# Up product of an MLP with its 192 channels as 128 + 64 contraction rows and the rests of two tiles in the two row halves of TensorE, and the projection bias added by GpSimd

## What is computed

```python
out = out.reshape(bw, WS, WS, DIM) @ proj_w + proj_b        # DIM = 192
out = window_unpartition(out, WS, pad_hw, (H, W))
x = shortcut + out
h2 = layernorm(x, n2_w, n2_b)
mlp = jax.nn.gelu(h2 @ lin1_w + lin1_b, approximate=False) @ lin2_w + lin2_b   # 192 -> 768 -> 192
return x + mlp
```

## Time and profile before

| | |
|---|---|
| three runs | 717.22, 715.27, 713.39 us, median 715.27 |
| the profiled execution | 715.34 us, of which 713.6 us from first to last instruction; TensorE's granted clock 0.979 on average |
| TensorE matmul | busy 642.6 us (90%), 5696 passes |
| TensorE weight loads | busy 492.6 us (69%), beside the matmuls |
| DVE, ACT, GpSimd | busy 359.8 (50%), 338.1 (47%), 112.8 us (16%) |
| up product, L544 | 192 passes, 87.1 us busy |

### The profile page before, as it was taken

How to read it: one execution, slowest core, us unless ns; L and a number is a source line. 1 busy time by engine, 2 the same in 40 slices (tenths; PEclk the granted TensorE clock), 3 DMA queues, 4 the chain that set the end, 5 groups by cost and what they waited for, 6 DMA issues and landing times.

```text
span 713.6 us, 14706 instructions
## 1 busy us (share of the span) xinstructions
PE 642.6 (90%) x5696; PEld 492.6 (69%) x5696; DVE 359.8 (50%) x982; ACT 338.1 (47%) x807; POOL 112.8 (16%) x156
## 2 busy tenths in 40 slices
PE   2889998999899989999999999999999977899996
PEld 2577757875787678767776777677767753676764
DVE  4466336633663466344734473547344713166665
ACT  3346543654365426542664266426642641254463
POOL 1500040004000400040004000400010021023130
PEclk9999999999999999999999999999999975999999
DMA  4673820085008400740073006300640000000000
GB/s 99 150 182 99 194 83 1 10 196 135 1 5 199 123 2 3 193 97 2 3 166 90 1 4 160 96 0 4 157 100 1 3 1 1 0 1 24 23 23 22
DMA packets 32954, 47.31 MB, mean 66 GB/s; under 512 B 5468, under 2 KB 13982, under 8 KB 32886
## 3 DMA queue, kind: packets, MB, share of 16 engines
q1 hardware_dynamic: 31654, 45.98, 26.5%
q10 hardware_dynamic: 1232, 0.40, 0.2%
HBM read 7.05 MB, written 1.57 MB: 12 GB/s over the span
## 4 chain that ended last, share of the span: by engine, by line
issue 58%; PE 22%; POOL 11%; DVE 5%; DMA 2%; ACT 2%; POOLq 0%; SPq 0%; ACTq 0%; DVEq 0%
PE bank L544 3%; POOL xn L735 3%; POOL q_nat L722 3%; PE bank L696 2%; PE bank L366 2%; POOL rstd L715 2%; PE bank L554 2%; PE bank L690 2%; PE bank L474 2%; PE bank L493 2%; POOL x_all L728 2%; PE bank L681 1%; PE bank L444 1%; PE bank L672 1%; DVE neg_max L877 1%
## 5 line engine op out<-in xcount | busy, mean ns | idle before, releaser
L1117 ACT ACTIVATE PT<-bank 98x392 f32<-98x392 f32 (+1 forms) x288 | 137.2, 491 | 152.0 <-PE bank L474 147.6
L877 DVE TENSOR_REDUCE neg_max<-bank 98x2 f32<-98x392 f32 x192 | 104.9, 561 | 111.7 <-PE bank L444 111.2
L474 PE MATMUL bank<-q_aug,k_aug 127*98 127x196 f32 (+1 forms) x672 | 112.5, 263 | 3.4 <-DMA q_aug<-negT 1.3
L444 PE MATMUL bank<-k_aug,q_aug 126*98 126x196 f32 x384 | 88.8, 317 | 9.8 <-DVE neg_max L877 9.0
L474 PEld LDWEIGHTS bank<-q_aug,k_aug 127*98 127x98 f32 (+1 forms) x672 | 87.5, 168 | 13.8 <-ACT PT L1117 8.1
L544 PE MATMUL bank<-yT,w_up 96*128 96x512 f32 x192 | 87.1, 611 | 1.0 <-ACT yT L1143 1.0
L722 POOL TENSOR_TENSOR q_nat<-st_q 96x392 f32<-96x392 f32 (+2 forms) x48 | 24.9, 546 | 357.1 <-DVE st_q L845 357.1
L554 PE MATMUL bank<-w_down,PT 128*128 128x192 f32 x384 | 76.8, 331 | 3.7 <-ACT PT L1148 3.7
L366 PE MATMUL bank<-xT,w_qkv 97*96 97x256 f32 (+2 forms) x272 | 76.3, 397 | 1.8 <-ACT xT L1054 1.4
L444 PEld LDWEIGHTS bank<-k_aug,q_aug 126*98 126x98 f32 x384 | 56.1, 167 | 25.0 <-DVE neg_max L877 16.0
L544 PEld LDWEIGHTS bank<-yT,w_up 96*128 96x128 f32 x192 | 37.4, 196 | 45.7 <-issue 44.2
(11 more groups left out here) (88 smaller groups left out, 864.3 us busy)
## 6 DMA issues: line engine op xcount, KB each, us to landing
q_aug<-st_q SPq DMA_DIRECT2D x64, 192.0 KB
k_aug<-st_k SPq DMA_DIRECT2D x64, 192.0 KB, 4.5
q_aug<-st_r SPq DMA_DIRECT2D x64, 168.0 KB
x_all<-in_x SPq DMA_DIRECT2D x4, 384.0 KB, 7.2
q_aug<-negT ACTq DMA_DIRECT2D x96, 1.5 KB
k_aug<-st_p SPq DMA_DIRECT2D x16, 74.2 KB, 2.3
w_up<-in_up_w SPq DMA_DIRECT2D x2, 576.0 KB
w_down<-in_down_w SPq DMA_DIRECT2D x4, 288.0 KB
```

Of the source, the lines that this page charges most:

```text
L444: last = t_.matmul(b[0:HALF, WIN * r:WIN * r + WIN], q_aug[0:NEG, h, c + HALF * r:c + HALF * r + HALF], k_aug[0:NEG, h, c:c + WIN], start= ...
L474: last = t_.matmul(b[0:keys, m * k:m * k + m], k_aug[0:NEG + 1, h, c + keys * k:c + keys * k + keys], q_aug[0:NEG + 1, h, c:c + m], start= ...
L877: ins = v.tensor_reduce(neg_max[0:HALF, slot(n, u), e:e + 5:4], b[0:HALF, 0:2 * WIN] .rearrange("p (r m) -> p r m", r=2), AX.X, ALU.max, n ...
L1117: s.activation(PT[0:rows, i % 8, 0:m], bank[2 + i % 2][0:rows, 0:m], ACT.Exp).then_inc(S["exp"], 1)
```

## The change

The channel groups for the MLP are now 0 to 127 and 64 to 191 (both 128 rows, 64 channels twice in yT). `up(n, p)` makes the hidden tiles 2p and 2p + 1 together, with four products of 512 tokens: tile a over channels 0 to 127, tile b over channels 64 to 191, then the rest of a (channels 128 to 191, which lie on partitions 64 to 127) and the rest of b (channels 0 to 63, on partitions 0 to 63). The first two contract over 128 rows and need the whole array; the last two contract over 64 rows each, in different row halves, and write different banks. The six tiles now have the banks 4, 3, 2, 5, 4, 3. The weights are laid out for this on the host.

The projection loses its row of ones. Its bias comes as a 128 x 192 tile b_proj by a broadcast load at the end of load_front, and GpSimd adds it to x after the first layer norm of that job (`add_projection_bias`). `add_proj` of the first tile waits for that addition (semaphore xb).

```diff
-UP_BANK = (4, 3)
+UP_BANK = (4, 3, 2, 5, 4, 3)
...
-        w_proj = [sb(f"w_proj{l}", [97, G, C]) for l in range(2)]
-        w_up = [sb(f"w_up{l}", [96, G, MLP]) for l in range(2)]
+        w_proj = [sb(f"w_proj{l}", [96, G, C]) for l in range(2)]
+        w_up = [sb(f"w_up{l}", [128, MC + MC // 2, 128]) for l in range(2)]
+        b_proj = [sb(f"b_proj{l}", [128, C]) for l in range(2)]
...
-        yT = sb("yT", [97, G, TOK])
+        yT = sb("yT", [128, 2, TOK])
...
-        LD_FRONT, LD_BACK, LD_STATIC = 16 * 4, 16 * 7, 16 * 3
+        LD_FRONT, LD_BACK, LD_STATIC = 16 * 5, 16 * 6, 16 * 3
...
                 load(w_rel[l][:, :], d["rel"][l], ld_front[l])
+                load(b_proj[l][:, :], d["proj_b"][l].rearrange("(a n) -> a n", a=1).broadcast_to([128, C]), ld_front[l])
...
                 for g in range(G):
-                    last = t_.matmul(bank[PROJ_BANK[t]][:, 0:C], yT[0:97 - g, g, 128 * t:128 * t + 128],
-                                     w_proj[l][0:97 - g, g, :], start=(g == 0), stop=(g == 1))
+                    last = t_.matmul(bank[PROJ_BANK[t]][:, 0:C], yT[0:96, g, 128 * t:128 * t + 128],
+                                     w_proj[l][:, g, :], start=(g == 0), stop=(g == 1))
...
-                        last = t_.transpose(bank[2 + g][0:96, 128 * t:128 * t + 128], xn[:, 1, t, 96 * g:96 * g + 96], ident[:, :])
+                        last = t_.transpose(bank[2 + g][:, 128 * t:128 * t + 128], xn[:, 1, t, 64 * g:64 * g + 128], ident[:, :])
...
-            def up(n, f):
+            def up(n, p):
+
                 l = layer(n)
-                if f == 0:
+                if p == 0:
                     need(pe, "x2_dve", n, 1)
                     need(pe, "x2_act", n, 1)
-                if f >= 2:
-                    need(pe, "gelu", n, f - 1)
-                for g in range(G):
-                    last = t_.matmul(bank[UP_BANK[f % 2]][:, :], w_up[l][:, g, 128 * f:128 * f + 128], yT[0:96, g, :],
-                                     start=(g == 0), stop=(g == 1))
-                last.then_inc(S["up"], 1)
+                if p == 2:
+                    need(pe, "gelu", n, 2)
+                to_a, to_b = bank[UP_BANK[2 * p]][:, :], bank[UP_BANK[2 * p + 1]][:, :]
+                t_.matmul(to_a, w_up[l][:, 2 * p, :], yT[:, 0, :], start=True, stop=False)
+                t_.matmul(to_b, w_up[l][:, 2 * p + 1, :], yT[:, 1, :], start=True, stop=False)
+                t_.matmul(to_a, w_up[l][64:128, MC + p, :], yT[64:128, 1, :], start=False, stop=True).then_inc(S["up"], 1)
+                t_.matmul(to_b, w_up[l][0:64, MC + p, :], yT[0:64, 0, :], start=False, stop=True).then_inc(S["up"], 1)
...
+            def add_projection_bias(n):
+                need(pool, "xn1", n, 1)
+                pool.wait_ge(ld_front[layer(n)], LD_FRONT)
+                g_.tensor_tensor(x(n), x(n), b_proj[layer(n)][:, :].unsqueeze(1).to_broadcast([128, TILES, C]), ALU.add)\
+                    .then_inc(S["xb"], 1)
...
             sum_q(0, 1)
+            add_projection_bias(0)
+            add_projection_bias(1)
...
                 if n + 2 < JOBS:
                     rsqrt(n + 2, 1)
                     normalise(n + 2)
+                    add_projection_bias(n + 2)
...
                 need(dve, "proj", n, t + 1)
+                if t == 0:
+                    need(dve, "xb", n, 1)
```

More of the change, by code:

```diff
@@ L130, in program @@
         w_rel = [sb(f"w_rel{l}", [96, 2 * RT * HG]) for l in range(2)]
-        w_proj = [sb(f"w_proj{l}", [97, G, C]) for l in range(2)]
-        w_up = [sb(f"w_up{l}", [96, G, MLP]) for l in range(2)]
+        w_proj = [sb(f"w_proj{l}", [96, G, C]) for l in range(2)]
+        w_up = [sb(f"w_up{l}", [128, MC + MC // 2, 128]) for l in range(2)]
         w_down = [sb(f"w_down{l}", [128, MC, C]) for l in range(2)]
+        b_proj = [sb(f"b_proj{l}", [128, C]) for l in range(2)]
         b_up = [sb(f"b_up{l}", [128, MC]) for l in range(2)]
         b_down = [sb(f"b_down{l}", [128, C]) for l in range(2)]
-        affine = [sb(f"affine{l}", [96, 4, G]) for l in range(2)]
+        affine = [sb(f"affine{l}", [128, 4, G]) for l in range(2)]
         stats = sb("stats", [128, 2, TILES, 6])
@@ L178, in program @@
                  "o_copy ot_mm inv_sum o_tok oT_mm oT_dve oT_act proj x1 x1b x2_mm x2_dve x2_act up gelu down out "
-                 "t_mm t_copy fwd xf_dve xf_act mix1 relu_act relu_dve mix2 over o2 inv fold unfolded").split()
+                 "xb t_mm t_copy fwd xf_dve xf_act mix1 relu_act relu_dve mix2 over o2 inv fold unfolded").split()
         S = {k: sem(k) for k in names}
@@ L242, in load_front @@
                 load(w_rel[l][:, :], d["rel"][l], ld_front[l])
+                load(b_proj[l][:, :], d["proj_b"][l].rearrange("(a n) -> a n", a=1).broadcast_to([128, C]), ld_front[l])
             def load_back(l):
[L245 to L246 removed]
+                load(w_proj[l][:, :, :], d["proj_w"][l].rearrange("(g p) n -> p g n", g=G), ld_back[l])
                 load(b_down[l][:, :], d["down_b"][l].rearrange("(a n) -> a n", a=1).broadcast_to([128, C]), ld_back[l])
                 load(b_up[l][:, :], d["up_b"][l], ld_back[l])
[L249 removed]
+                load(w_up[l][:, :, :], d["w_up"][l], ld_back[l])
                 load(w_down[l][:, 0:3, :], d["down_w"][l].rearrange("(g p) n -> p g n", g=MC)[:, 0:3, :], ld_back[l])
@@ L646, in _ @@
                         pad_values_in(n + 1)
-                for f in range(MC):
-                    up(n, f)
+                for p in range(MC // 2):
+                    up(n, p)
                 if more:
@@ L839, in place_x @@
                 for dst, src in pieces(xT[0:96, 0, 0:TOK], bank[front_bank(n, "x0")][0:96, :]):
-                    last = v.tensor_scalar(dst, src, affine[l][:, 0, 0:1], affine[l][:, 1, 0:1], ALU.mult, ALU.add)
+                    last = v.tensor_scalar(dst, src, affine[l][0:96, 0, 0:1], affine[l][0:96, 1, 0:1], ALU.mult, ALU.add)
                 last.then_inc(S["xT_dve"], 1)
@@ L1053, in place_x @@
                 for dst, src in pieces(xT[0:96, 1, 0:TOK], bank[front_bank(n, "x1")][0:96, :]):
-                    last = s.activation(dst, src, ACT.Identity, bias=affine[l][:, 1, 1:2], scale=affine[l][:, 0, 1:2])
+                    last = s.activation(dst, src, ACT.Identity, bias=affine[l][0:96, 1, 1:2], scale=affine[l][0:96, 0, 1:2])
                 last.then_inc(S["xT_act"], 1)
@@ L1142, in place_y @@
                 need(act, "x2_mm", n, 2)
-                s.activation(yT[0:96, 1, :], bank[3][0:96, :], ACT.Identity, bias=affine[l][:, 3, 1:2],
+                s.activation(yT[:, 1, :], bank[3][:, :], ACT.Identity, bias=affine[l][:, 3, 1:2],
                              scale=affine[l][:, 2, 1:2]).then_inc(S["x2_act"], 1)
@@ L1147, in gelu @@
                 need(act, "up", n, f + 1)
-                s.activation(hidden[:, f, :], bank[UP_BANK[f % 2]][:, :], ACT.Gelu, bias=b_up[layer(n)][:, f:f + 1])\
+                s.activation(hidden[:, f, :], bank[UP_BANK[f]][:, :], ACT.Gelu, bias=b_up[layer(n)][:, f:f + 1])\
                     .then_inc(S["gelu"], 1)
@@ L1367 @@
              [get(f"L1_conv_{k}") for k in ("ln1_g", "ln1_b", "ln2_g", "ln2_b")]]
-    arrays["affine"] = np.array(norms).reshape(2, 4, G, 96).transpose(0, 3, 1, 2)
+    norms = np.array(norms)
+    arrays["affine"] = np.zeros((2, 128, 4, G), np.float32)
+    arrays["affine"][:, 0:96, 0:2] = norms[:, 0:2].reshape(2, 2, G, 96).transpose(0, 3, 1, 2)
+    arrays["affine"][:, :, 2:4] = np.stack([norms[:, 2:4, 0:128], norms[:, 2:4, 64:192]], axis=-1).transpose(0, 2, 1, 3)
+    w = arrays.pop("up_w").reshape(2, C, MC, 128)
+    even, odd = w[:, :, 0::2], w[:, :, 1::2]
+    w_up = np.empty((2, 128, MC + MC // 2, 128), np.float32)
+    w_up[:, :, 0:MC:2], w_up[:, :, 1:MC:2] = even[:, 0:128], odd[:, 64:192]
+    w_up[:, 0:64, MC:], w_up[:, 64:128, MC:] = odd[:, 0:64], even[:, 128:192]
+    arrays["w_up"] = w_up
     arrays["up_b"] = arrays["up_b"].reshape(2, MC, 128).transpose(0, 2, 1)
```

7 lines of the change are left out of this document (3 added, 4 removed).

## The result

| | before | changed |
|---|---|---|
| median of six executions each | 714.77 us (711.5 to 717.2) | 705.83 us (703.4 to 709.2) |
| ratio, with its interval | | 0.9874 (0.9839 to 0.9908) |
| profiled execution, span | 715.34, 713.6 us | 709.21, 707.4 us |
| one period of a job | 71.71 us | 70.68 us |
| first up pass to last up pass | 9.87 us | 8.30 us |

The changed kernel is 8.9 us (1.3%) faster; forecast were 5.3. Most executions of both kernels fall into two groups about 4.5 to 5 us apart (703.4 to 704.0 and 707.7 to 709.2 changed; 711.6 to 713.7 and 716.3 to 717.4 in the set of before that the first four experiments used, with one more at 723.6), and the mean granted clock says which: 0.978 or more in the lower, 0.976 or less in the upper, to which the profiled execution of the change belongs. A period is the time from the first up product of one job to that of the next.

A forecast was written before the change was run, and what follows sets the result against it. TensorE was taken as the bound, busy 67.55 of a 71.7 us period. The sum 7 x (1.36 - 0.71) + 0.8 = 5.3 us less than 715.34 gave 710.0 us, with an 8 in 10 range of 703 to 719 us.

The forecast's parts named there:

- rival C: Up stage: row halves have cheap edges; 700.4 us, or 705 with half the edges gone; chance 0.13 (below 706).
- Passes: Up stage: both rests overlap fully in two slots, saving 0.86 us a pair, 2.57 us a job.
- Rival A: Up stage: passes start strictly in order, seven slots a pair; 717.0 us; chance 0.15 with its softer form.
- B: Up stage: row halves run one behind the other, eight slots plus edges; 725.0 us, slower; chance 0.10.
- Edges: Up stage: each switch between whole and divided array costs 0.20 us, two a pair, 0.40 us.
- The second Gelu: End of up stage: both last tiles finish together, so down waits 0.71 us more per job, all on the path.
- The last job: Its up stage begins at half clock for some 6.8 us; gains 1.5, loses 0.71: 0.8 us.
- Things at nothing: Transposes, evictions, projection, GpSimd's eight additions and the b_proj load were each taken to cost nothing.

The follow-up runs named there:

- the first four experiments: Follow-ups run 1 to run 4 on the changed kernel's up stage, compared with the kernel before at 716.74 us (17 executions).
- run 1: Changed kernel with both rests of a pair in the same row half (rows 64 to 127): 726.29 us, ratio 1.015 to the kernel before.
- run 2: Changed kernel with the rests as products over all 128 rows, so no divided array: 712.21 us, ratio 0.9974 to the kernel before.
- run 3: Changed kernel with each pair's two rests ahead of its whole-array products: 700.38 us, ratio 0.9789 to the kernel before.
- run 6: The changed kernel once more, unaltered: 704.51 us, ratio 0.9876 to the kernel before.
- run 4: Changed kernel with all six rests of a job in one group and six banks: 694.5 us, ratio 0.9687 to the kernel before.
- Run 8: run 4's version with 9 unread products in gaps at the start and 28 in the last job's gaps: 688.32 us, ratio 0.9645 to the kernel before.

## Why the prediction was right, and where its sum was off

The direction and the mechanism were right, and 705.83 us lies in the range. The gain was sized at 5.3 us and measured 8.9, in the medians and in the trace from the first up product on. By the time alone it might be rival C with part of the edges gone, since 705.83 lies just below the 706 to 713 that the forecast claimed for itself. The runs say that the edges are there and that other terms were off, all of them towards too small a gain. The low end of that band was also wider than its own condition: 48 edges of 0.15 instead of 0.20 us give 707.6, not 706.

- **Passes.** "Both rests in two slots" holds: the four starts above, and run 1 as the counterpart. Rivals A and B fall with it. For A, L549's first pass starts 0.53 us ahead of L548's second. Had the passes kept the order of the products, the time would have been 717.0 us. The Trainium skill (TensorE: Matmul & The Clock Gate, Part 3, The mechanism) says that matmuls start and end in strict order, and for the products as wholes the trace agrees: first passes at 171.54 and 171.55, last passes both at 172.08. Rival A carried that order over to the single passes, and there it doesn't hold.
- **Edges.** Estimated at 0.20 us from a stage with column groups; run 2 against run 1 gives 0.98 for five. A pair was put at 2.98 us and measures 2.97. Rival C falls.
- **The edge that is not on the path.** The first error: I charged every pair with two edges, the third too. But its way out lies in the gap in which down waits for Gelu; no pass of the up stage stands behind it. 0.20 us a job were charged for nothing. The changed kernel's stage says so by itself: 17 slots of 0.43 and five edges of 0.20 are its 8.30 us. The stage, from the first up pass to the end of the last, shrank by 1.57 us and not by 1.36.
- **The second Gelu.** The second error: 0.71 us was the distance from a Gelu's start to ACT's next, dissimilar instruction. With its input ready a second Gelu starts 0.57 to 0.585 us behind the first, each 0.68 us long, so the start of one overlaps the end of the other. That is 0.14 us a job. The place and the kind of the loss were right: 1.94 instead of 1.37 us, and run 3 wins it back.
- The two together turn the forecast 0.65 us a job into the 1.00 measured: 7.0 instead of 4.6 us in seven jobs. The periods gained 7.3; the 0.3 us beyond the stages aren't traced to a cause.
- **The last job.** Put at 0.8 us, measured 1.6 in the profiled execution and 2.1 in run 6. It was worked out with 6.8 us at half clock, as in the profile of before; in the profile of the change the clock was full again after 5.7:

```profile
593.70:599.40 5.70, 5.70 (x9) 0.50 0.01 3
599.40:605.20 5.80, 5.80 (x18) 1.00 0.00 0
```

How long that lasts isn't given by the program: the stage took 11.12 us in one execution of the changed kernel and 10.60 in the other. The same holds without the change. Run 2 has the up stage of the kernel before and took 12.24 + 1.37 us in the last job, where the profile of before has 13.29 + 1.37. Set against run 2 the gain is 0.6 or 1.1 us. So this term lies between 0.6 and 2.1 us, and the runs don't settle it more closely.
- **Things at nothing.** GpSimd's additions, the transposes, evictions, projection and loads: right, by run 2's period. Down's wait was forecast 5 us longer in sum and grew by 3.4, which is the second error again. It is less than 8 x 0.57 because the edge out of the divided array uses part of the gap: the scores in it end 1.12 us behind the start of the last up pass (178.03 to 179.15) where they ended 0.96 behind the earlier trace rows. Only the last job, which has no scores there, shows the whole 0.57.
- **The start.** Not in the sum. It moved the profiled execution by 2.8 us against the change (4.5 by the clock, less the 1.8 by which the profile of before was late), and run 6 shows that the change isn't its cause.

What stays open: why the start runs at half clock for 3.4 us in one execution of the changed kernel and for 17 in another (0 in the profiles of runs 1 and 3, 13.7 in that of run 4), and what decides how long the last job's stretch lasts. Run 8 shows only that products in the gaps keep the clock full. The two executions of run 4 with the highest clock weren't profiled.

## What to carry to other kernels

A wait at the end of a stage absorbs what lies between the last instruction that feeds it and the waiting one: count an edge, a drain or a load only if something on the path stands behind it. When two tiles are made to end together, their consumer works them off one after the other behind the stage; let them end apart, and put divided and undivided stretches of the array in as few changes as the banks allow (six rests in one go saved 0.6 us of edges a job against three pairs, and the last two tiles ending apart another 0.57). Look at the granted clock of a stage at the end of a program, where no other work fills the gaps, before tuning the stage: 28 useless products brought 6 us there.

## What the runs showed of the hardware that I had not expected

- Two products in the two row halves run fully side by side, both passes of each: starts 0.01 us apart, second passes 0.53 us later.
- A change between whole and divided array costs 0.20 us at 128 stationary columns: the first pass behind it starts 0.52 instead of 0.43 us after the one before, and the second 0.53 us after the first (171.02, 171.54, 172.08).
- Two Gelus of 128 x 512 from PSUM start 0.585 us apart at a recorded length of 0.684 us, four take 2.42 us.
- TensorE stayed at its lower level, 1.2 GHz, through 17 us without a gap in run 1's last job. In the stretch from 590 to 601 us before it, it had been busy for 6.6 of 11 us. The same stage of the changed kernel ran at 0.76 in the mean, by this row:

```profile
593.60:605.60 12.00, 11.71 (x24) 0.76 0.00 1
```
